# Offsets of a deformable-convolution network as pairs of 16-bit parts: one spreading matmul in place of two, the clip on VectorE and the shift on GpSimd

## What is computed

```python
h = relu(deconv2d(x, dc_w, dc_b))
offset = conv2d(h, of_w, of_b)
x = relu(deform_conv2d(h, offset, dw, db))   # 4 times; inputs are summed in pairs
...
x_cat = concatenate((x, in_module))
out = x_in + deform_conv2d(x_cat, conv2d(x_cat, fin_off_w, fin_off_b), fin_dcn_w, fin_dcn_b)
```

## Time and profile before

| | |
|---|---|
| median of three runs | 4319.1 us (4306.77 to 4320.78) |
| span of the profiled execution, first to last instruction | 4314.1 us |
| mean granted TensorE clock | 0.940 of full speed |
| TensorE (matmul) / VectorE / ScalarE / GpSimd busy | 3880.1 / 2952.5 / 2786.4 / 1140.5 us |
| spreading matmuls L544 | 21,504, 1745.6 us busy |
| GpSimd L1103 and L1105 | 320 each, 366.3 and 769.6 us busy |

### The profile page before, as it was taken

The page is one execution under the profiler, slowest core; times in us unless marked ns, Lnnn a source line. Parts: engine busy times, 40 slices in busy tenths (PEclk is TensorE's granted clock), DMA queues, the critical chain, the costliest instruction groups (busy, mean ns, idle before and its releaser), DMA issues.

```text
span 4314.1 us, 221726 instructions
## 1 busy us (share of the span) xinstructions
PE 3880.1 (90%) x81908; PEld 2973.5 (69%) x81908; DVE 2952.5 (68%) x5858; ACT 2786.4 (65%) x6651; POOL 1140.5 (26%) x645
## 2 busy tenths in 40 slices
PE   4998799699789879979988997998799999799998
PEld 3776577477567657756765775776577777577776
DVE  5885687488567668847856884784577774577775
ACT  2885588388478658837865883885355554255554
POOL 0441243134033214403322431331111110111111
PEclk8999899799989989989998997999799999899999
DMA  4442544344244334424424443443766664666664
GB/s 125 127 127 66 143 125 110 89 126 127 75 132 126 90 106 127 125 76 131 126 71 127 127 114 92 126 125 109 179 154 152 150 150 127 147 154 152 152 150 110
DMA packets 244838, 533.50 MB, mean 124 GB/s; under 512 B 61200, under 2 KB 151824, under 8 KB 227216
## 3 DMA queue, kind: packets, MB, share of 16 engines
q1 hardware_dynamic: 194224, 498.67, 45.0%
q10 hardware_dynamic: 50240, 29.89, 2.4%
HBM read 471.87 MB, written 56.45 MB: 122 GB/s over the span
## 4 chain that ended last, share of the span: by engine, by line
PE 68%; SPq 18%; issue 7%; ACT 2%; DMA 2%; DVE 2%; POOLq 0%; ACTq 0%; DVEq 0%; POOL 0%; PEld 0%; PEldq 0%
PE P L544 26%; PE PS L562 24%; SPq L380 9%; PE P L515 8%; PE PS L575 8%; SPq L388 8%; SPq L370 1%; PE PS L515 1%; ACT H L848 1%; DMA X<-x_dram 1%; PE P L530 1%; DVE FOFF L1032 1%; DMA VT<-ht_store 0%; DVE A L917 0%; DVE ST L1036 0%
## 5 line engine op out<-in xcount | busy, mean ns | idle before, releaser
L917 DVE TENSOR_TENSOR A<-P,YC 121x384 f32<-121x384 f32 (+1 forms) x4608 | 2311.4, 550 | 850.1 <-ACT YC L768 684.5
L544 PE MATMUL P<-HL,SEL 32*121 32x384 f16 (+1 forms) x21504 | 1745.6, 304 | 131.6 <-issue 95.3
L768 ACT ACTIVATE YC<-P 121x384 f32<-121x384 f32 (+1 forms) x4608 | 1733.9, 444 | 98.7 <-PE P L544 65.8
L544 PEld LDWEIGHTS P<-HL,SEL 32*121 32x121 f16 (+1 forms) x21504 | 1126.9, 117 | 513.9 <-issue 228.6
L562 PE MATMUL PS<-A,VT 121*32 121x80 f32 (+1 forms) x40960 | 1342.7, 250 | 51.7 <-DMA VT<-ht_store 15.5
L562 PEld LDWEIGHTS PS<-A,VT 121*32 121x32 f32 (+1 forms) x40960 | 1093.0, 117 | 354.6 <-issue 200.4
L1103 POOL CAST HL<-DIST 128x1152 f16<-128x1152 f32 x320 | 366.3, 1145 | 3066.1 <-DVE DIST L922 3043.8
L745 ACT ACTIVATE SMP<-PS 128x480 f32<-128x480 f32 (+3 forms) x1152 | 593.9, 516 | 638.2 <-PE PS L562 632.9
L1105 POOL TENSOR_TENSOR HL<-DIST,HL 128x1152 f16<-128x1152 f32 x320 | 769.6, 2405 | 58.5 <-POOL HL L1103 58.5
L735 ACT ACTIVATE DIST<-HB,CONST 128x1152 f32<-128x1152 f32 x320 | 400.8, 1252 | 231.4 <-DMA HB<-off_store 128.8
L575 PE MATMUL PS<-SMP,CW 128*64 128x128 f32 x7424 | 476.0, 277 | 5.4 <-ACT SMP L745 5.4
(11 more groups left out here) (61 smaller groups left out, 703.4 us busy)
## 6 DMA issues: line engine op xcount, KB each, us to landing
HB<-off_store SPq DMA_DIRECT2D x2560, 72.0 KB
VT<-ht_store SPq DMA_DIRECT2D x256, 512.0 KB
VT<-ht_store SPq DMA_DIRECT2D x768, 132.0 KB
VT<-ht_store SPq DMA_DIRECT2D x256, 88.0 KB
off_store<-FOFF SPq DMA_DIRECT2D x160, 128.0 KB, 2.6
H<-x_dram SPq DMA_DIRECT2D x5, 2048.0 KB, 14.6
ht_store<-A ACTq DMA_DIRECT2D x32, 256.0 KB, 3.3
ht_store<-VT ACTq DMA_DIRECT2D x32, 256.0 KB, 3.9
```

What stands on the lines that cost most here:

```text
L544: mm = nc.tensor.matmul(dst, SEL[q, table, 0:sh.npos], hats, start=part == 0, stop=part == 1)
L768: nc.scalar.activation(YC[0:sh.npos, g % X_SLOTS, 0:sh.size], P[0:sh.npos, g % Y_SLOTS, 0:sh.size], ACT.Copy).then_inc(y_ready, 1)
L917: return nc.vector.tensor_tensor(dst, x, y, ALU.mult)
```

## The change

Offsets are now scaled by 2048 x 2048 in FOFF, and each is split into two 16-bit integers, a high part (in units of 1/2048 of a pixel) and a low part that carries the rest together with the high part's fraction of a pixel. Both parts of one coordinate stand in one 32-row quadrant: 16 rows for the high part, 16 for the low part, of the same axis. The columns of a chunk's HB, CLIP and HL hold all 18 coordinates (2,304 columns of 16 bits in place of 1,152 f32), so that one matmul over 32 rows adds up both parts: `spread` has one matmul where it had two, and SEL holds differences of neighbouring rows.

- Distance (ScalarE), clamp (VectorE) and the two hats operations (GpSimd) become one `clip` on VectorE (L969, minimum and maximum with a bound per partition, 16-bit to 16-bit) and one operation on GpSimd (L1175, add and multiply with a value per partition, to f16). The clip of chunk c+1 follows product 5 of chunk c and waits for the shift of chunk c.
- In setup, GpSimd makes the high part of each item in two operations (L1184, L1190) and VectorE the low part in three (`split`, L1092 to L1098). The split of item n-1 follows the raw part of item n. SyncE stores the parts (`store_parts`, two DMAs an item of 512 runs of 256 bytes), and the f32 FOFF, which only the fallback reads, is stored by ScalarE (`store_far`).
- 38 semaphores are cleared in place of 30; SEL is made by four operations in place of two; ScalarE's copy to YC scales by 1 / (2048 x 2048).

```diff
-            def store_offsets(n):
+            def store_parts(n):
                 unit, image = divmod(n, IMG)
-                sp.wait_ge(off_ready, n + 1)
+                sp.wait_ge(parts_ready, n + 1)
                 for top in range(2):
-                    at = (8 * unit + 4 * top) * BAND_SIZE + image * 2 * CH * CPX
-                    dst = bass.AP(off_store.ap().tensor, at, [[CPX, 2 * CH], [BAND_SIZE, 4], [1, CPX]])
-                    sp.dma_start(dst, FOFF[64 * top:64 * (top + 1), n % OFF_SLOTS, :].rearrange(
+                    at = (image * BANDS + 8 * unit + 4 * top) * W_BAND
+                    dst = bass.AP(part_store.ap().tensor, at, [[CPX, 2 * CH], [2 * CH * CPX, 8], [1, CPX]])
+                    sp.dma_start(dst, FPART[64 * top:64 * (top + 1), n % OFF_SLOTS, :].rearrange(
                         "p (q x) -> p q x", x=CPX)).then_inc(off_stored[n % OFF_SLOTS], 16)
...
                 def next_offsets(c, band, half):
-                    sp.wait_ge(abs_done, c - 1)
+                    sp.wait_ge(clip_done, c - 1)
                     load_offsets(band, half)
...
-            def spread(sh, g, b, par, table, out, column=0):
+            def spread(sh, g, b, par, axis, table, out, column=0):
...
-                for part in range(2):
-                    hats = HL[q, part, par, 3 * CPX * third:3 * CPX * (third + 1)]
...
-                    mm = nc.tensor.matmul(dst, SEL[q, table, 0:sh.npos], hats, start=part == 0, stop=part == 1)
+                at = (TAPS * axis + 3 * third) * CPX
+                hats = HL[q, par, at:at + 3 * CPX]
...
+                return nc.tensor.matmul(dst, SEL[q, table, 0:sh.npos], hats, start=True, stop=True)
...
-            def distance(band, half):
-                wait_alone(act, hb_full[half], 32 * IMG * (band + 1))
-                nc.scalar.activation(DIST[:, :], HB[:, half, :], ACT.Abs, bias=HAT_BIAS).then_inc(abs_done, 1)
...
+                def store_far(n):
+                    unit, image = divmod(n, IMG)
+                    act.wait_ge(off_ready, n + 1)
+                    for top in range(2):
...
+                        act.dma_start(dst, FOFF[64 * top:64 * (top + 1), n % OFF_SLOTS, :].rearrange(
+                            "p (q x) -> p q x", x=CPX)).then_inc(far_stored[n % OFF_SLOTS], 16)
...
-            def clamp(c):
-                dve.wait_ge(abs_done, c + 1)
-                nc.vector.tensor_scalar(DIST[:, :], DIST[:, :], SCALE, SCALE, ALU.min, ALU.subtract).then_inc(clamp_done, 1)
+            def clip(c, band, half):
+                dve.wait_ge(hb_full[half], 32 * IMG * (band + 1))
+                nc.vector.tensor_scalar(CLIP[:, :], HB[:, half, :], RAMP_HIGH, RAMP_LOW, ALU.min, ALU.max).then_inc(clip_done, 1)
...
-                            if b == 0 and g == sh.next_at + 1 and not last:
-                                clamp(c + 1)
+                            if b == 0 and g == sh.sum_after + 4 and not last:
+                                dve.wait_ge(hats_full, c + 1)
+                                clip(c + 1, band + half, 1 - half)
...
+                def split(n):
+                    dve.wait_ge(whole_done, n + 1)
+                    nc.vector.scalar_tensor_tensor(by_band(FINE[:, n % 2, :]), off_part(n, 0), -SCALE, by_band(FOFF[:, n % OFF_SLOTS, :]),
+                                                   ALU.mult, ALU.add).then_inc(fine_done, 1)
+                    nc.vector.tensor_scalar(by_band(COARSE[:, n % 2, :]), off_part(n, 0), -2048, None,
+                                            ALU.bitwise_and).then_inc(coarse_done, 1)
+                    dve.wait_ge(fine_done, n + 1)
+                    dve.wait_ge(coarse_done, n + 1)
+                    nc.vector.scalar_tensor_tensor(off_part(n, 1), by_band(FINE[:, n % 2, :]), 1.0, by_band(COARSE[:, n % 2, :]),
+                                                   ALU.mult, ALU.add).then_inc(parts_ready, 1)
+
+                for n in range(ITEMS):
+                    raw_offsets(n)
+                    if n > 0:
+                        split(n - 1)
+                split(ITEMS - 1)
...
             def hats(c, half):
-                wait_alone(pool, clamp_done, c + 1)
-                nc.gpsimd.tensor_copy(HL[:, 0, half, :], DIST[:, :]).then_inc(hat_step, 1)
-                wait_alone(pool, hat_step, c + 1)
-                nc.gpsimd.tensor_tensor(HL[:, 1, half, :], DIST[:, :], HL[:, 0, half, :], ALU.subtract).then_inc(hats_full, 1)
+                wait_alone(pool, clip_done, c + 1)
+                nc.gpsimd.tensor_scalar(HL[:, half, :], CLIP[:, :], RAMP_SHIFT, RAMP_WEIGHT, ALU.add,
+                                        ALU.mult).then_inc(hats_full, 1)
+
+            def split(n):
+                pool.wait_ge(off_ready, n + 1)
...
+                nc.gpsimd.tensor_scalar(WHOLE, FOFF[:, n % OFF_SLOTS, :], 1.0 / SCALE, MAGIC, ALU.mult,
+                                        ALU.add).then_inc(whole_step, 1)
+                pool.wait_ge(whole_step, n + 1)
...
+                nc.gpsimd.tensor_scalar(off_part(n, 0), by_band(WHOLE), -MAGIC, 1.0, ALU.add,
+                                        ALU.mult).then_inc(whole_done, 1)
```

More of the change, by code:

```diff
@@ L12 @@
 I32 = mybir.dt.int32
+I16 = mybir.dt.int16
 LAYERS = 4
@@ L100, in __init__ @@
         self.runs = {g: range(e + 1, g + 1) for e, g in zip([-1, *ends], ends)}
-        self.next_at = 0 if kind == 0 else self.after[0]
         self.lag = 3 - self.batches
@@ L608, in spread_x @@
                         for tile, table in enumerate(x_tables):
-                            mm = spread(sh, g, b, half, table, Y_SLOTS + g % X_SLOTS, sh.size * tile)
+                            mm = spread(sh, g, b, half, 1, table, Y_SLOTS + g % X_SLOTS, sh.size * tile)
                         mm.then_inc(x_full, 1)
@@ L752, in read_sum @@
                     out_act(layer, PS[:, :], half, final).then_inc(ps_free, 1)
-                def next_distance(c, band, half):
-                    wait_alone(act, hats_full, c)
-                    distance(band, half)
                 def body(c, band, half, before, last):
@@ L762, in body @@
                             n = (c * sh.batches + b) * sh.ngr + g
-                            if sh.kind == 0 and g == sh.next_at and not last:
-                                next_distance(c + 1, band + half, 1 - half)
                             act.wait_ge(y_full, n + 1)
@@ L788, in tail @@
                     read_sum(CHUNKS - 1, 1)
+                    for slot in range(OFF_SLOTS):
+                        wait_alone(act, far_stored[slot], 32 * ITEMS // OFF_SLOTS)
                 chunk_loop(act, body, tail)
@@ L852, in step @@
                     for unit in range(UNITS):
+                        if unit == 1:
+                            for n in range(IMG):
+                                store_far(n)
                         keep_transposes(0, unit)
@@ L855, in step @@
                             store_ht(unit, n)
-                distance(0, 0)
+                    for n in range(IMG, ITEMS):
+                        store_far(n)
                 sampling(act, bar_count, final, lambda sh: body_of(sh, layer, final),
@@ L1058, in step @@
                 flag_count[0] += 1
-                clamp(0)
+                clip(0, 0, 0)
                 chained()
@@ L1116, in step @@
             def step(layer, group, bar_count, final):
+                for n in range(ITEMS):
+                    split(n)
                 hats(0, 0)
@@ L1147, in _tables @@
     consts[:, 6:10] = -1e30
-    consts[row < TAPS, 6:8] = 0.0
-    consts[(row >= AXIS) & (row < AXIS + TAPS), 8:10] = 0.0
+    consts[row < TAPS, 6:8] = [HALF_STEP, -HALF_STEP]
+    consts[(row >= TAPS) & (row < COORDS), 8:10] = [HALF_STEP, -HALF_STEP]
     consts[:, 10:14] = [BOUND1, BOUND1 - 3.0, BOUND1, BOUND1 - 3.0]
+    start = SCALE * (q - MARGIN) - np.where(low_part, HALF_STEP, 0.0)
+    full = np.where(low_part, SCALE, SCALE - 1.0)
+    consts[:, 14] = np.where(last, start, start + full)
+    consts[:, 15] = start
+    consts[:, 16] = np.where(last, full, 0.0) - start
+    consts[:, 17] = np.where(low_part, 1.0 / SCALE, 1.0)
     far = np.zeros((128, CPX + CHUNKS + 16), np.float32)
```

167 lines of the change are left out of this document (111 added, 56 removed).

## The result

The changed kernel takes 4610.6 us (median of 4 runs, 4603.1 to 4613.9) against 4319.6 us: a ratio of 1.068, 95% interval 1.066 to 1.070. The profiled execution has a span of 4612.0 us, 298 us over that of before; 79 were forecast. The time lies in the range given, on the side forecast, and at nearly four times the distance.

A forecast was written before the change was run, and what follows sets the result against it. SyncE's load issues, 8.55 us a chunk, were taken to bound layer-step sampling. Setup +81 and +23, clears +5, slack -16, spreads -14 gave +79 us: 4393 span, 4398 us median; 8-in-10 range 4320 to 4680.

The forecast's parts named there:

- The setup: Offset split, stores and loads before sampling, ending with SyncE: +81 us over eight layer steps, +23 us over two final steps.
- The final steps: Sampling there: the turnaround hides most of the halved spreads; 0.2 us of each of 62 periods, -14 us (0 to -22).
- SyncE's floor: Layer-step sampling: SyncE's queue issues loads without rest, so no chunk period falls below its 8.55 us.
- The step that failed: Layer-step sampling: engines' loop of 8.2 to 8.4 us stays under SyncE's 8.55, so no steady gain and no loss.
- The clock: TensorE's clock in sampling: granted in full; a fall to the lower level was possible and counted under the first rival.
- the first rival: Layer-step sampling: GpSimd's shift becomes the bound, from 2.3 to 2.45 us on; about 4700 us at 3.5; chance 0.28.
- The loop's length: A layer-step chunk's loop of shift, spreads, sums, products and clip: 6.1 to 6.3 us plus the shift, 8.2 to 8.4.
- The slack gain of 16 us: Last chunks of each layer step follow their loads closer: 2 us for each of eight steps, -16 us (0 to -26).
- H: Length of GpSimd's shift, one operation on 2,304 elements a chunk: taken as 2.13 us, up to 4.8 us possible.
- The two other rivals: Faster, SyncE's issues no floor: 4278 or 4228 us, chance 0.12. No change, smaller setup growth: 4330 us, chance 0.10.
- The weighing of the shared port: VectorE and GpSimd excluding each other in SBUF: judged not shown by the trace; by the rule an estimated +30 us.
- The two figures for GpSimd: One-input work at 1.03 or about 1.8 cycles an element; by the second the shift takes an estimated 3.5 us.

The follow-up runs named there:

- e11: The changed kernel with the clip behind product 3 and the 16-bit stores of items 4 to 7 issued by ScalarE's queue instead of SyncE's; 4358.7 us, ratio 1.010.
- e6: The changed kernel with the clip behind product 3 instead of product 5; 4389.9 us, ratio 1.018.
- e8: The changed kernel, clip late, GpSimd's shift cut to its first 1,152 columns in all but a step's first two chunks (output wrong); 4392.5 us, ratio 1.018.
- e1: The changed kernel with the clip behind product 1 instead of product 5; 4397.1 us, ratio 1.020.
- e9: The changed kernel with the clip behind product 3 and half of the offset loads issued by GpSimd; 4186.6 us, ratio 0.970.
- e4: The kernel before with SyncE's eight offset loads of a chunk merged to four of 32 rows each, same bytes; 5804.7 us, ratio 1.345.
- e2: The changed kernel, clip late, with every spreading matmul issued twice into the same place; 4804.9 us, ratio 1.114.
- e3: The changed kernel, clip late, with two of a chunk's spreads repeated (six and five times more) just ahead of TensorE's two pauses; 4618.9 us, ratio 1.071.
- e7: The changed kernel with the clip behind product 1 and every spreading matmul issued twice; 4447.1 us, ratio 1.031.

## Why the prediction was right and wrong

**The setup: right.** +10.1 and +11.5 us a step were worked out from SyncE's order; the trace gives 40.3 us from the first item to the last load where 39.5 was forecast, and +115 us over ten steps where +109 was. e11 took the stores out of that chain and got 3.3 us a step back. The stores of 512 runs took 0.69 us each (5.54 / 8) behind the loads, under the 0.98 taken, which is 2.3 us less for eight; the loads behind item 3's stores went out 4.6 us after these (474.99 + 12.63 to 492.25) where 1.9 was taken for the landing, 2.7 us more. The path was right; that its two errors made up was luck.

**The final steps: right in sign, too small.** -24.5 us for -14, past the end of -22; 0.31 us a chunk instead of 0.2 (0.2 x 62 is 12.4, not 14).

**SyncE's floor: right, but not reached.** e6 and e8 came to rest at 8.6 us (as did e1, which has a second bound there), and e9 lowered the floor and the period with it. That the floor bound the kernel before is read from its trace and from e4, which made the queue heavier; no run made it lighter there. It doesn't bind the changed kernel.

**The step that failed** is the sentence "With 2.13 the loop is 8.2 to 8.4 us, just under SyncE's 8.55: no steady gain and no loss." In its place the chain of clip and shift became longer than SyncE's issues and set a mean period of 9.55 us. Three things were wrong in it, by size:

- *The clock.* The prediction priced the loop at the full clock, and put a lower one into the first rival without a price ("No row shows that with TensorE at work without long pauses"). But the loop it drew has TensorE wait for the shift in every chunk. Where the clock was lower the loop is 10.05 us, and the mean period is 9.55, 0.77 above the loop's 8.78; over 248 periods that is 190 us. What the lower level costs could be read from the kernel before (lines below).
- *The loop's length.* 8.78 us at the full clock, not 8.2 to 8.4: the shift 0.14 and the clip 0.12 us longer; the other 0.1 to 0.3 us lie in the terms between them and weren't taken apart. Against the 8.62 of before this is 0.16 us, 40 us in all.
- *The slack gain of 16 us* needs the loop below SyncE's pace, and so went with it. With the clip early the layer steps' sampling was 8 us shorter than before.

In the kernel before, sampling after the first setup began at the lower clock (0.50 up to 116 us) and had the full one from 120 us on (1.00):

```profile
114.08 1.83 PE L562 MATMUL PS<-A,VT 121*32 121x80 f32 x48
115.83 1.56 PE L544 MATMUL P<-HL,SEL 32*121 32x384 f16 x12
...
119.03 0.89 PE L544 MATMUL P<-HL,SEL 32*121 32x384 f16 x12
...
124.41 1.04 PE L562 MATMUL PS<-A,VT 121*32 121x80 f32 x48
```

Samples and spreads took 1.75 times as long at the lower level. So the price of a lower clock was there to be read; that it would fall in the new loop was not.

The split between clock and length is arithmetic on the trace's short and long chunks; no run kept the late clip and the full clock. The two together, 0.93 x 248 = 231 us, are more than the 206.6 us by which the layer steps' sampling grew, since chunks 6 to 26 stand for all: over all 31 periods the mean went from 8.67 to 9.54 us, 216 us, and the stretch ahead of a step's first sums is about 1 us shorter.

The first rival's mechanism came true, at a chance of 0.28, but not through its condition: it was to decide from H = 2.3 to 2.45 us, and H was 2.27. The margin of 0.2 us between loop and floor was too thin to give the other side half of the chance. The two other rivals didn't come: setup grew by all that was counted, and SyncE's queue was a floor.

**The weighing of the shared port was wrong.** The prediction read the residual's 0.61 us across the cast as its usual length. Alone it takes 0.344 us (the changed kernel); in the kernel before the group's mean is 559 ns:

```profile
L911 DVE SCALAR_TENSOR_TENSOR X<-X,CONST,TMP 128x128 f32 x280 | 156.4, 559 | 0.0
```

At 194.60 + 0.61 = 195.21 it ended 0.14 us behind the cast's end (195.07), as it ended 0.15 us behind the shift's in e1. This is no chance: 232 of the 320 residuals of the kernel before overlap the cast, and each ended 0.14 to 0.16 us behind it; the other 88 took 0.34 to 0.36 us. In e1 232 overlap the shift and end 0.14 to 0.15 us behind it. What the Trainium skill says in "SBUF — State Buffer" (Who interferes with whom), that a VectorE operation with two inputs in SBUF and a GpSimd operation that reads SBUF exclude each other, agrees with both. In the change itself it cost nothing: the late clip keeps the residual clear of the shift, and in setup the split ran at 0.69 to 0.71 us beside GpSimd's operations, which were done by then.

**The two figures for GpSimd.** The shift's 2,267 ns are 0.91 ns an element after the cast's 0.16 us fixed. Of the two figures for one input that "GPSIMD Engine Reference" (section 3.1) of the Trainium skill gives, the first, 1.03 cycles (an estimated 0.86 ns at the 1.2 GHz that the section reckons with), is near it; 1.8, by which the shift would be an estimated 3.5 us, is not.

## What to carry to other kernels

Where a step is taken out of an engine's way, ask which chain becomes the longest at the *lower* clock too: a loop in which TensorE waits once a round may be priced at its full clock only if it stays clear of the bound by more than the lower clock costs. A margin of 2% between two bounds is a coin's toss, not a forecast; the place of one 0.9 us instruction in VectorE's order (behind product 3 or behind product 5) was worth 220 us here, and the cure for a queue that issues without rest was to give part of its issues to an engine that idles (7.71 us a chunk for 8.63). A short instruction's length has to be compared with its length alone, not with its neighbours': the residual's wait for GpSimd stands inside the instruction (1.37 us for 0.34 in e1).

## What the runs showed that was not expected

- The granted clock fell in sampling loops in which TensorE was busy for 83% (the change, 560 to 740 us), 92% (e2) and 98% (e3) of the time, to 0.89 to 0.90, and was 0.99 to 1.00 in others at 97% to 99% (e9, e7). What it follows wasn't settled.
- One DMA for 32 rows, made of two groups of repeated rows, took SyncE 1.8 to 2.1 us to issue; two for 16 rows each take 0.96 us together.
- GpSimd issued a load in 0.49 us (1.95 us for four), as fast as SyncE, and issued next to its own work without slowing it (shift 2.26 us).
